# Vision tower on one Trainium2 core: where two of five groups of transposes stand in the expert stages

## The reference

```
topk_scores, topk_idx = jax.lax.top_k(gate_scores, K)          # K = 2 of 8 experts
topk_probs = jax.nn.softmax(topk_scores, axis=-1)
combine = jnp.sum(topk_probs[..., None] * jax.nn.one_hot(topk_idx, E, dtype=x.dtype), axis=-2)
for e in range(E):
    h = jax.nn.relu(jnp.einsum('bsd,hd->bsh', x, W1[e]) + b1[e])
    y = jnp.einsum('bsh,dh->bsd', h, W2[e]) + b2[e]
    out = out + combine[..., e:e + 1] * y
```

## Time and profile before

| | us |
|---|---|
| median of 3 runs | 1307.79 (1307.03 to 1307.94) |
| the profiled execution | 1313.2 |
| its span, first to last instruction | 1311.0 |
| its mean granted clock of TensorE | 0.915 of full speed |
| first expert stage, first to last L1230 product | 359.4 to about 660 |
| second expert stage, first to last L1230 product | about 955 to 1291.9 |

### The profile page before, as it was taken

The page is one execution under the profiler, slowest core; times in us unless marked ns, Lnnn a source line. Parts: engine busy times, 40 slices in busy tenths (PEclk is TensorE's granted clock), DMA queues, the critical chain, the costliest instruction groups (busy, mean ns, idle before and its releaser), DMA issues. The chain is left out here.

```text
span 1311.0 us, 25470 instructions
## 1 busy us (share of the span) xinstructions
PE 1149.6 (88%) x8586; PEld 855.8 (65%) x8586; DVE 916.7 (70%) x2212; ACT 590.0 (45%) x1147; POOL 430.3 (33%) x592
## 2 busy tenths in 40 slices
PE   6778576888599999999939796998799999999996
PEld 2344575766477777777728454776777777777774
DVE  1566655677567777777748786996468877887774
ACT  1233574111256555655523343776154555455542
POOL 2111000111114343444433456873003333433334
PEclk9899799667599999999979898999589999999998
DMA  8200000000000000000000000000000000000000
GB/s 203 100 0 0 1 0 0 1 0 0 0 1 1 1 1 1 1 1 1 1 0 1 1 1 1 2 2 3 0 1 6 6 11 6 7 6 11 7 6 11
DMA packets 3439, 13.28 MB, mean 10 GB/s; under 512 B 400, under 2 KB 2192, under 8 KB 3088
## 3 DMA queue, kind: packets, MB, share of 16 engines
q1 hardware_dynamic: 3056, 7.92, 2.3%
q0 software_dynamic: 288, 4.11, 0.8%
HBM read 9.89 MB, written 2.13 MB: 9 GB/s over the span
## 5 line engine op out<-in xcount | busy, mean ns | idle before, releaser
L1230 PE MATMUL moe_psU<-moe_nT_parts,moe_w_hi 128*128 128x320 f32 x988 | 324.8, 339 | 2.0 <-DVE moe_hid L1140 1.1
L1230 PE MATMUL moe_psU<-moe_nT_parts,moe_w_lo 128*128 128x320 f32 x988 | 296.7, 310 | 0.0
L1230 PEld LDWEIGHTS moe_psU<-moe_nT_parts,moe_w_hi 128*128 128x128 f32 x988 | 188.1, 190 | 56.8 <-issue 50.3
L1230 PEld LDWEIGHTS moe_psU<-moe_nT_parts,moe_w_lo 128*128 128x128 f32 x988 | 188.8, 191 | 0.0
L1134 DVE TENSOR_TENSOR moe_hid<-moe_psU,moe_silu 128x320 f32<-128x320 f32 x286 | 139.2, 491 | 62.2 <-ACT moe_silu L998 54.1
L925 POOL TENSOR_TENSOR moe_sum<-moe_scaled 128x256 f32<-128x256 f32 x130 | 99.1, 762 | 171.4 <-DVE moe_scaled L1124 170.7
L998 ACT ACTIVATE moe_silu<-moe_psU 128x320 f32<-128x320 f32 x286 | 125.3, 439 | 56.9 <-PE moe_psU L1230 43.1
L1003 ACT ACTIVATE moe_hid<-moe_psU,middle 128x320 f32<-128x320 f32 x260 | 129.2, 526 | 33.3 <-PE moe_psU L1230 31.0
L1140 DVE TENSOR_SCALAR moe_hid<-moe_psU,middle 128x320 f32<-128x320 f32 x156 | 85.6, 550 | 64.8 <-PE moe_psU L1230 64.0
L1241 PE MATMUL moe_psY<-moe_hid,late 128*64 128x320 f32 x832 | 123.4, 439 | 0.9 <-DVE moe_hid L1134 0.9
L1241 PE MATMUL moe_psY<-moe_hid,middle 128*64 128x320 f32 x832 | 123.5, 439 | 0.7 <-ACT moe_hid L1003 0.7
(11 more groups left out here) (299 smaller groups left out, 2111.4 us busy)
## 6 DMA issues: line engine op xcount, KB each, us to landing
images<-in_x SPq DMA_DIRECT2D x8, 576.0 KB, 14.1
late<-in_late POOLq DMA_DIRECT2D x1, 2456.5 KB, 12.0
out_tokens<-h SPq DMA_DIRECT2D x13, 160.0 KB, 1.8
middle<-in_middle POOLq DMA_DIRECT2D x1, 1554.0 KB, 6.9
early<-in_early SPq DMA_DIRECT2D x1, 962.5 KB, 23.0
early<-in_early SPq DMA_DIRECT2D x1, 80.0 KB, 2.1
```

Of the source, the lines that this page charges most:

```text
L1230: last = pe.matmul(psum[:, 0:HALF], w[:, col:col + SPLIT], moving, start=(part == 0), stop=(part == 1))
```

## The change

Two turn groups per tile change places, in both stages: t = 1 and t = 3 go behind the down group, to k = `DOWN` of pairs 1 and 2. In the second stage t = 4 goes one unit further too, from (2, 2) to (2, 3). In the first stage the weighings of t = 1 and 3 go to the place after, k = 5. In the second stage `WEIGH` is `OUTS`, so they are at k = 1, where the small steps are too.

```diff
@@ -893,15 +893,15 @@
         if layer == 0:
             LOGITS, DOWN = (0, 2), 4
-            OUTS = [(0, 7), (1, 2), (1, 7), (2, 2), (2, 6)]
+            OUTS = [(0, 7), (1, 4), (1, 7), (2, 4), (2, 6)]
             TURN = [(3, 2)]
-            WEIGH = [(0, 7), (1, 3), (1, 7), (2, 3), (2, 7)]
+            WEIGH = [(0, 7), (1, 5), (1, 7), (2, 5), (2, 7)]
...
         else:
             LOGITS, DOWN = (0, 0), 1
-            OUTS = [(0, 3), (1, 0), (1, 3), (2, 0), (2, 2)]
+            OUTS = [(0, 3), (1, 1), (1, 3), (2, 1), (2, 3)]
```

## The result

The changed kernel takes **1356.3 us** (median of 6 runs, 1353.7 to 1363.6) against 1307.9 of the kernel before (6 runs on the same chip, 1306.6 to 1312.0). The ratio is 1.038, with a 95% interval of 1.035 to 1.042: slower by 46 to 54 us. The forecast was slower, 1347, range 1333 to 1361. The time lies in the range, 9 us above the forecast, and that difference needs a reason: the sum was 39 us and the loss is 48. The time also lies above the bounds of the sum, which end at 1355; the range reached 1361 only for waits of the first stage, and these did not come.

A forecast was written before the change was run, and what follows sets the result against it. TensorE was taken to bound the kernel, with DVE having 5 us to spare per tile. 3.39 us in eleven tiles is 37.3, with the twelfth 39.2; 1307.8 + 39.2 = 1347 us, range 1333 to 1361.

The forecast's parts named there:

- waits of the first stage: Rival: the first stage's 0.4 us cover fails, TensorE waits 0.3 twice a tile, 7.2 us, 1354; chance 0.09.
- small steps of pair 1, to the eviction: Second stage, DVE: seven steps behind the weighing take 2.08 us until the eviction of (1, 2), 2.34 in the kernel before.
- gate side of (1, 5) starts, its wait: Second stage, TensorE: wants the bank of (1, 2) at 5.33, gets it at 6.36, waits 1.03 us.
- second wait at (2, 1): Second stage, TensorE: wants the bank of (1, 4) at 7.64, free at 7.85, waits 0.21 us.
- cost of pair 1: Second stage: next down group at 8.35 instead of 6.90 without waits, 1.45 us a tile.
- small steps of pair 2, to the eviction: Second stage, DVE: the steps behind the weighing take 2.27 us until the eviction of (2, 2), 2.53 in the kernel before.
- wait at L1199: Second stage, pair 2: L1199 at 6.95 waits for the weighing of t = 4 until 7.56, 0.61 us.
- cost of pair 2: Second stage: next down group at 8.09 instead of 6.15 without waits, 1.94 us a tile.
- at their present length: Bound: second-stage small steps not shortened, 0.26 us more twice a tile, +5.7 us.
- The clock rival: Rival: clock falls to half behind each second-stage wait, 2 us 24 times, 47 on top, about 1394; chance 0.06.
- The first stage and TensorE's own work: First stage covered by 0.4 us, cost 0; moved turn groups taken as 0, 4.8 us either way over 48 groups.
- The other side, the delay absorbed: Rival: DVE reaches the second stage's eviction of (1, 2) by 4.70 us, TensorE does not wait, 1303; chance 0.07.

The follow-up runs named there:

- e1: The changed kernel with the second stage's small steps ahead of the weighing on DVE, TensorE's list as changed: 1308.4 us, ratio 0.999.
- e11: The changed kernel with the second stage's turn groups on TensorE early again as before the change, DVE's list as changed: 1314.5 us, ratio 1.007.
- e2: The kernel before with the first stage's moves alone, second stage unchanged: 1309.0 us, ratio 1.000.
- e7: The changed kernel with POOL's first two sums behind each second-stage weighing cut from 256 and 128 columns to 4: 1327.5 us, ratio 1.015.
- e9: The changed kernel with eight silu products added at (3, 1) of the second stage alone, filling that wait: 1354.3 us, ratio 1.037.
- e10: The changed kernel with eight silu products added at (1, 5) of the second stage alone, filling that wait: 1362.0 us, ratio 1.043.
- e6: The kernel before with t = 3 and t = 4 of the second stage alone moved, to (2, 1) and (2, 3): 1345.7 us, ratio 1.030.

## Why the prediction was right in kind and short in size

Point by point, times from the start of the down group, forecast and measured. The prediction counted waits from start to start, and so they are measured here; the profile's own numbers for the three long ones are 1.23, 1.36 and 0.53.

| step | forecast | measured |
|---|---|---|
| turn group behind the down group | 2.30 | 2.31 |
| weighing | 3.05 | 3.00 |
| first small step | 3.65 | 3.61 |
| small steps of pair 1, to the eviction | 2.08 | **2.55** |
| eviction of (1, 2) | 5.73 | 6.16 |
| gate side of (1, 5) starts, its wait | 6.36, 1.03 | 6.70, 1.39 |
| second wait at (2, 1) | 0.21 | 0.11 |
| next down group; cost of pair 1 | 8.35; 1.45 | 8.58; 1.71 |
| small steps of pair 2, to the eviction | 2.27 | **2.73** |
| gate side of (3, 1) starts, its wait | 6.55, 1.22 | 6.83, 1.52 |
| wait at L1199 | 0.61 | 0.68 |
| next down group; cost of pair 2 | 8.09; 1.94 | 8.47; 2.32 |

The costs of the pairs are taken against 6.87 and 6.15, what the same list of TensorE takes in e1.

**The mechanism was right.** The idle time stands at the predicted products, ended by the predicted operations, and e1 shows that the order on DVE is all of it: with the same list of TensorE and the steps first, nothing is lost. With the turn group early, in e11, that order costs 0.45 us a tile; the 3.97 need both.

**The term that was mis-sized is the length of the small steps.** The prediction took 0.26 off their present length, by L1051 directly behind a weighing in the first stage (0.48 against 0.81). L1051 did come at 0.48. But the 0.81 had been stretched by POOL's sum, and in the new place the sums only fall on other steps: L1095 took 0.73 instead of 0.45, and L1097 and L1098 0.37 instead of 0.20. Each chain came out 0.46 to 0.47 longer than forecast. The working looked at one row where the operation stands in its new place, and not at what POOL would be doing beside the six behind it, though the change moved the start of POOL's sums too. Even the bound "at their present length", +5.7, was too low: the steps took 0.21 more than the 2.34 of pair 1 and 0.20 more than the 2.53 of pair 2.

Of the 0.93 us by which the two chains exceed the forecast, other terms took a part back. The first small step came 0.04 sooner in each pair, and from the eviction's start to the product it released went 0.54 and 0.49 us, not 0.63. The second wait was 0.10 shorter, and L1199 lost 0.10 more. The pairs cost 0.26 and 0.38 more than forecast, 3.39 + 0.64 = 4.03; the tile as a whole grew by 3.97, in eleven tiles 43.7 us instead of 37.3. That the sum of the forecast missed by no more is in part luck: most of these smaller errors went the other way. And the range holds the result only because it was widened past its own bounds for a rival that did not come.

**The second wait at (2, 1) came**, as a late load of 0.22 us: the product starts 0.11 late and the one behind it 0.10 more.

**The clock rival came in part.** It had 0.06 and 47 us on top, at both waits in all tiles; it came behind (3, 1) alone, in 4 of 11 tiles, for 6.7 us. The prediction named a falling clock as a sign that it is wrong, and on this point it was: those four tiles have 0.95 in the mean. The row against it (1.14 us of idle time and then full speed) holds for the wait at (1, 5), 1.23, behind which the clock never fell. It says nothing on two waits two products apart. The Trainium skill (TensorE: Matmul & The Clock Gate, A second HAM failure mode) tells of a clock that oscillates by small idle times between groups of matmuls; the trace agrees with it for the 1.36 and 0.53 at (3, 1), and not for the wait at (1, 5).

**The first stage and TensorE's own work** were forecast at 0, and e2 measures 0 within 0.3%. Two moved groups make the tile 0.08 us shorter in the first stage and 0.04 in e1's second, 1.4 us in 24 tiles where 4.8 either way were allowed. The turn group's weighing came at 0.69 instead of 0.75:

```profile
497.60 0.65 PE L1252 MATMUL moe_psM<-early,moe_y 128*128 128x128 f32 x4
...
498.29 0.69 DVE L1124 TENSOR_TENSOR moe_scaled<-moe_psM,moe_weights 128x512 f32<-128x512 f32 x1 [0.76 <-PE moe_psM L1252]
```

**The other side, the delay absorbed,** decided at 4.70 us for the eviction of (1, 2); it came at 6.16. Even e7, with steps of 1.68, has it at 5.29 and waits 0.36.

Together: 39.2 forecast, 6.4 more in eleven tiles, 0.3 less in the twelfth (1.6 instead of 1.9) and 6.7 for the clock make 52.0 in the second stage, and the first gives 1.1 back. That is 51, and the medians differ by 48.4, with 46 to 54 as their interval.

## What to carry to other kernels

Where an engine works its list in order, look at what stands behind an operation that will have to wait: small work ahead of the wait stays hidden, and the same work behind it made the evictions late that free the banks, 4 us a tile here. When you take a duration for an operation in its new place, look at what the other engines will be doing beside it and behind it, and not only at one row of the same operation elsewhere; and ask of the old row too whether it was the operation's own length. A short wait can have a second price where another follows close behind: here the clock fell in some tiles, and unneeded products in the wait were then cheaper than idle time (7.6 us between e9 and e10).

## What the runs showed of the hardware

- Small DVE operations with two SBUF inputs are stretched by a sum of POOL that began ahead of them: 0.19 to 0.73 us beside a sum of 128x256, 0.20 to 0.37 beside the smaller ones, each to an end 0.05 or 0.06 behind the sum's, and the chain of seven from 1.68 to 2.55. One that began first kept its 0.48, and the sum took 0.91 instead of 0.73. A reduction wholly beside a sum stayed at 0.20 (L1096 of before).
- TensorE's clock fell behind waits of 1.36 and 0.53 us two products apart, in 4 of 11 tiles (7 of 11 in e6), and never behind the single waits of 1.23 and 1.60, or behind 0.52 with the first one filled. A down group then took 3.44 to 3.94 us instead of 2.37.
- Eight more products of 128x320 in a wait of 1.36 us cost nothing in the tile (30.19 against 30.18).
- A wait that the profile gives as 1.23 us delays the next product by 1.39, and a delay of 0.11 shows in the row of the weight load alone (e11's 0.28 is 0.44 in the same way).
